# The first layer norm of a two-layer network in pairs of row tiles, with another order of the products behind it

## The reference, cut to what matters

```python
def _layernorm(x, axis=-1, eps=1e-05):
    m = jnp.mean(x, axis=axis, keepdims=True)
    v = jnp.var(x, axis=axis, keepdims=True)
    return (x - m) / jnp.sqrt(v + eps)
...
x = L0_attn_x
xn = _layernorm(x, axis=-1)
s = _L0_attn_ref(xn, ...)                 # q, k, v projections, softmax attention
g = _silu(_L0_ffn_ref(xn, ...))           # 16 experts, the top 4 of each row
x = x + s * g
...                                       # a second layer of the same build
```

## Time and profile before

| what | value |
|---|---|
| time, median of 3 runs | 410.19 us (410.18 to 410.86) |
| the profiled execution | 410.36 us |
| its span, first to last instruction | 408.6 us |
| TensorE busy | 392.9 us, 96% |
| VectorE, ScalarE, GpSimd busy | 315.1, 231.4, 210.3 us |
| chain that ended last | TensorE 85%, VectorE 11% |

### The profile page before, as it was taken

One profiled execution on the slowest core, in us unless ns is written; L12 is line 12 of the kernel. 1 busy time (PEld: TensorE's weight loads), 2 busy tenths in 40 slices (PEclk: granted clock), 3 DMA queues, 4 the chain that ended last, 5 costly groups with the idle time before them and its releaser, 6 DMA issues.

```text
span 408.6 us, 9640 instructions
## 1 busy us (share of the span) xinstructions
PE 392.9 (96%) x3063; PEld 289.1 (71%) x3063; DVE 315.1 (77%) x1070; ACT 231.4 (57%) x583; POOL 210.3 (51%) x205
## 2 busy tenths in 40 slices
PE   8999999999999999999899899999999999999995
PEld 4846797797787787566576677468778776566784
DVE  5895888888897556698999988766877862645895
ACT  3463334434344446899999943645777767524731
POOL 1214487776763210486878410177777620677710
PEclk9999999999999999999999999999999999999999
DMA  6949789899999997288788973034656544233322
GB/s 214 391 205 319 249 294 300 277 296 314 291 321 290 309 316 254 64 191 231 137 207 206 270 263 131 13 92 130 197 178 189 163 150 135 80 104 103 91 72 70
DMA packets 41361, 82.84 MB, mean 203 GB/s; under 512 B 6960, under 2 KB 26288, under 8 KB 40672
## 3 DMA queue, kind: packets, MB, share of 16 engines
q1 hardware_dynamic: 30080, 60.59, 44.3%
q0 software_dynamic: 9600, 19.93, 19.4%
q10 hardware_dynamic: 1632, 1.71, 1.3%
HBM read 65.42 MB, written 14.68 MB: 196 GB/s over the span
## 4 chain that ended last, share of the span: by engine, by line
PE 85%; DVE 11%; issue 3%; ACT 1%; ACTq 0%; DVEq 0%
PE ps L1261 13%; PE ps L1200 8%; PE ps L1485 7%; PE ps L1300 6%; PE ps L1406 5%; PE ps L1227 5%; PE ps L1379 4%; PE ps L1496 3%; PE ps L1256 3%; PE ps L1186 3%; PE ps L1029 3%; PE ps L1048 2%; PE ps L1045 2%; PE ps L1238 2%; PE ps L1387 2%
## 5 line engine op out<-in xcount | busy, mean ns | idle before, releaser
L592 POOL DMA_INDIRECT til<-xn_rows,gidx x64 | 62.5, 976 | 82.7 <-PE ps L1238 37.2
L915 ACT ACTIVATE til<-til,mxs 128x128 f32<-128x128 f32 (+1 forms) x128 | 48.9, 451 | 0.0
L1261 PEld LDWEIGHTS ps<-til,experts 128*128 128x128 f32 x384 | 45.4, 192 | 4.2 <-DVE til L1832 2.4
L1261 PE MATMUL ps<-til,experts 128*128 128x128 f32 x384 | 47.7, 277 | 0.4 <-DVE til L1832 0.3
L767 ACT ACTIVATE til<-ps 128x256 f32<-128x256 f32 x40 | 15.3, 382 | 56.5 <-PE ps L1238 55.6
L1956 DVE CUSTOM_DVE_ANT_0 til<-ps,cst 128x128 f32<-128x128 f32 (+1 forms) x128 | 37.9, 354 | 5.2 <-PE ps L1379 4.5
L816 ACT ACTIVATE til<-ps,wtile 128x256 f32<-128x256 f32 x88 | 38.7, 469 | 4.3 <-PE ps L1229 2.4
L1202 PE MATMUL ps<-xn,til 128*64 128x192 f32 x192 | 33.8, 329 | 0.0
L1200 PE MATMUL ps<-experts,til 128*64 x192 | 33.7, 329 | 0.0
L1300 PE MATMUL ps<-experts,til 128*128 x128 | 33.1, 381 | 0.0
L1406 PE MATMUL ps<-cst,til 128*128 128x128 f32 x192 | 27.5, 280 | 4.2 <-DVE til L1965 3.0
(11 more groups left out here) (278 smaller groups left out, 1034.8 us busy)
## 6 DMA issues: line engine op xcount, KB each, us to landing
experts<-in_gu SPq DMA_DIRECT2D x32, 512.0 KB, 5.4
sorted_rows<-til SPq DMA_DIRECT2D x88, 128.0 KB, 4.2
att<-in_gu SPq DMA_DIRECT2D x16, 512.0 KB
experts<-in_gu SPq DMA_DIRECT2D x8, 768.0 KB
experts<-in_dn SPq DMA_DIRECT2D x4, 1024.0 KB, 11.2
experts<-in_dn SPq DMA_DIRECT2D x8, 384.0 KB
experts<-att SPq DMA_DIRECT2D x44, 32.0 KB
xn_rows<-xn ACTq DMA_DIRECT2D x8, 128.0 KB, 4.8
```

The lines of the kernel that those rows point to most:

```text
L592: po.indirect_dma_start(to, None, xn_dram[s.n], bass.IndirectOffsetOnAxis(ap=gidx[:, at:at + 1], axis=0))\
L915: ins = ac.activation(pr[h % len(pr)][:, cols], pr[h % len(pr)][:, cols], ACT.Exp, bias=mxs[:, h % len(pr), tt:tt + 1], scale=-1.0)
L1261: mm = pe.matmul(ps[:, b0, m * P:(m + 1) * P], gw[n][:, k * w + m * P:k * w + (m + 1) * P], xgT[:, j % 2, k, :], start=(k == 0), stop=(k = ...
```

## The change

The norm of the first layer goes by pairs of tiles. VectorE takes the statistics of the next pair between the moments of a pair and its normalisation, the last two pairs being written out apart. Epsilon is no longer added by VectorE: it is a column of its own (`eps`, set by a new memset ahead of `ones_bf`) that ScalarE adds as the bias of its root, read straight from the variances. ScalarE takes four roots of two tiles in place of two of four; the second, third and fourth stand behind its copies of tiles 0, 2 and 3. On TensorE 11 products of ones run in place of 16, `router(3)` stands ahead of `narrow(0)` and `turn(4)`, and `narrow(6)` ahead of `count(3)`. The table's first use writes to a scratch column instead of `rstd`.

```diff
@@ scalar
-            ac.wait_ge(s_dve, 1)
-            ac.activation(rstd[:, 0:1], ones_e[:, 0:1], ACT.Sqrt)
+            ac.wait_ge(s_dve, 2)
+            ac.activation(ahead[:, :], ones_e[:, 0:1], ACT.Sqrt)
...
+                    def deviations(b):
+                        ac.wait_ge(s.ve_ready, b + 1)
+                        ac.activation(sd[:, 2 * b:2 * b + 2], mv[:, 2 * b:2 * b + 2, 1], ACT.Sqrt, bias=eps[:, :]).then_inc(s.sd_ready, 1)
+
+                    deviations(0)
                     for i in range(NTT):
-                        if i % 4 == 0:
-                            ac.wait_ge(s.ve_ready, i // 4 + 1)
-                            ac.activation(sd[:, i:i + 4], sd[:, i:i + 4], ACT.Sqrt).then_inc(s.sd_ready, 1)
                         turned(s, i)
+                        if i in (0, 2):
+                            deviations(i // 2 + 1)
+                        if i == 3:
+                            deviations(3)
@@ tensor
                         if i == 4:
+                            router(s, 3)
                             narrow(s, 0)
                         if i < NTT:
                             turn(s, i)
-                        if i >= 1:
+                        if i >= 1 and i != 4:
                             router(s, i - 1)
...
                     narrow(s, 5)
+                    narrow(s, 6)
                     count(s, 3)
-                    narrow(s, 6)
                     narrow(s, 7)
...
-            dense(16, 2)
+            dense(11, 2)
@@ vector
+            def pair_stats(b):
+
+                if b < len(X_PARTS):
+                    ve.wait_ge(s_x[b], 16)
+                for i in (2 * b, 2 * b + 1):
+                    ins = ve.bn_stats(bnst[:, i, :], xr[:, i, :])
                 link(ins)
...
+            def pair_moments(b):
+
+                for i in (2 * b, 2 * b + 1):
                     ins = ve.bn_aggr(mv[:, i, :], bnst[:, i, :])
...
+                ins.then_inc(L[0].ve_ready, 1)
+
+            def pair_normal(b):
+
+                ve.wait_ge(L[0].sd_ready, b + 1)
+                link(ve.reciprocal(rstd[:, 2 * b:2 * b + 2], sd[:, 2 * b:2 * b + 2]))
+                ve.wait_ge(L[0].ve_ready, b + 1)
+                for i in (2 * b, 2 * b + 1):
                     ve.tensor_scalar(xn[:, i, :], xr[:, i, :], mv[:, i, 0:1], rstd[:, i:i + 1], ALU.subtract, ALU.mult)\
-                      .then_inc(s.xn_ready, 1)
+                      .then_inc(L[0].xn_ready, 1)
...
             link(ve.memset(ones_e[:, :], 1.0))
+            link(ve.memset(eps[:, :], EPS))
             ve.memset(ones_bf[:, :], 1.0).then_inc(s_cbf, 1)
-            variances(L[0], 0)
-            rows_normal(L[0], 0, 4, 1)
-            variances(L[0], 1)
-            rows_normal(L[0], 4, NTT, 2)
+            pair_stats(0)
+            pair_moments(0)
+            for b in (0, 1):
+                pair_stats(b + 1)
+                pair_normal(b)
+                pair_moments(b + 1)
+            pair_stats(3)
+            pair_moments(3)
+            pair_normal(2)
+            pair_normal(3)
```

More of the change, by code:

```diff
@@ L239, in build_program @@
         bnst = sb("bnst", [P, NTT, 6])
+        eps = sb("eps", [P, 1])
         mv = sb("mv", [P, NTT, 2])
@@ L1577, in _ @@
             done = {}
[L1579 to L1585, removed]
+            def pair_stats(b):
[3 more added lines that the diff above has]
+                    ins = ve.bn_stats(bnst[:, i, :], xr[:, i, :])
                 link(ins)
-                for i in range(4 * h, 4 * h + 4):
+            def pair_moments(b):
+                for i in (2 * b, 2 * b + 1):
                     ins = ve.bn_aggr(mv[:, i, :], bnst[:, i, :])
[L1589 to L1596, removed]
+                ins.then_inc(L[0].ve_ready, 1)
[4 more added lines that the diff above has]
+                for i in (2 * b, 2 * b + 1):
                     ve.tensor_scalar(xn[:, i, :], xr[:, i, :], mv[:, i, 0:1], rstd[:, i:i + 1], ALU.subtract, ALU.mult)\
-                      .then_inc(s.xn_ready, 1)
+                      .then_inc(L[0].xn_ready, 1)
             def picks(s, p):
```

## The result

The changed kernel took 416.87 us (median of six executions, 413.93 to 419.96) against 410.19 before: a ratio of 1.0151, with a 95% interval of 1.0116 to 1.0186, which is 4.8 to 7.6 us slower. The direction was forecast; 412.2 was not reached by any execution, and the median lies 3 us above the range. The six executions of this one program are 6 us apart (413.93, 414.51, 414.70, 419.04, 419.92, 419.96), while those of before lay within 0.8 us. The mean granted clock is 0.990 to 0.996 in the three faster ones and 0.977 to 0.978 in the three slower. The profiled execution is the fastest, 413.93 (span 412.1, and 1.8 around it). Of the runs further down, two executions in the chip's slower state, 567 us of e10 and 453 us of the kernel before beside it, are left out of every median.

The account below looks back on a forecast made before the run. TensorE, busy 96% of the span, was taken as the bound: 1.1 us later at `narrow(1)` plus 0.86 for `narrow(6)` made 410.36 + 1.96 = 412.32, less 0.17 for the median: 412.2 us, range 410.6 to 413.9.

Parts of the forecast that it names:

- Starvation and order: Late rows and TensorE's new order delay `narrow(1)` about 1.1 us, `narrow(6)` adds 0.86: 1.96 us; chance 0.63.
- the hinge: End of `count(3)` on TensorE, which starts `nts` at 18.97; any delay there delays everything behind it equally.
- The range of this case: Main forecast of waits and order on TensorE: 1.3 to 2.6 us slower, given as 411.5 to 412.9 us.
- the two stops at the routers: TensorE waits 0.2 us before `router(3)` and 0.4 us before `router(4)` in the new order.
- The root with a bias: ScalarE's first root, bounded by 0.20 and 0.39 us, ends before VectorE needs it, so it is hidden.
- Rival 2: Tile 2 reaches TensorE by about 7.1, so TensorE is not starved: 409.9 us, or within 0.2%; chance 0.20.
- The warming products: Before TensorE's first turn: eleven products run from 1.36 to about 5.8 us, where sixteen ended at 6.68.
- Part 2: With eleven products TensorE is free for tile 0 at 6.02 and turns it at 6.09, 0.68 us earlier.
- rival 1: TensorE's clock rises later or falls again after fewer products and idle time: up to 1.5 us more, 413.7; chance 0.17.
- The sign that the prediction named for this: Router or `narrow` rows between 8 and 13 us spaced twice as far as before would mean the clock.
- Near 20.9: Start of `nts` on VectorE after the change, in place of 18.97, with VectorE idle about 2.3 us before it.

Follow-up runs that it names:

- e10: Changed kernel with rows in four transfers, second root before ScalarE's first copy, TensorE's old order, 11 products plus 4 after `turn(1)`: 409.81 us, ratio 0.9989.
- e1: Changed kernel with 16 warming products in place of 11, all else as changed: 412.61 us, ratio 1.0056.
- e4: Changed kernel's pairs and bias with 16 warming products and TensorE's order of before: 411.27 us, ratio 1.0016.
- e7: Kernel before with only `narrow(6)` moved ahead of `count(3)`: 411.12 us, ratio 1.0016.
- e8: Changed kernel with 16 products and rows fetched in four transfers, the third ahead of the identity matrix: 413.10 us, ratio 1.0059.
- e9: Kernel before with 11 products, plus 24 products of 16 columns before the first turn and 16 between `turn(1)` and `router(0)`: 414.94 us, ratio 1.0083.
- e6: Kernel before with its 16 products divided, 11 ahead of the first turn and 5 between `turn(1)` and `router(0)`: 411.87 us, ratio 1.0009.
- e2: Kernel before with 11 warming products in place of 16, nothing else: 417.38 us, ratio 1.0151.
- e0: The changed kernel once more, unaltered, on another chip: 418.31 us, ratio 1.0169.
- e5: Changed kernel with its 11 products plus four more between `router(0)` and `turn(2)`: 412.75 us, ratio 1.0058.

## Why the prediction was half right

**Starvation and order: right.** Point by point in the trace of after: VectorE idles 0.74 us before its third statistics (0.65 forecast) because of the transfer of rows; the third tile is turned at 8.63 (8.66); the last choice, at 18.28, ends before TensorE is there, so `narrow(6)` lies in front of the hinge. e1 has the sum without the clock, 2.3 us by its ratio (1.6 to 3.0) for 1.96 forecast. (The range of this case, +1.3 to +2.6 on 410.19, ends at 412.8 and not at 412.9; nothing hangs on it.) e4 and e7 have two of its parts, 0.7 us each by their ratios (0.1 to 1.3, and none to 1.3), for 0.54 and 0.86, though the clock fell in both profiles and is mixed into these times; the two stops at the routers, 0.55 by the forecast, were not tried alone.

**The root with a bias: right.** ScalarE's row of after, against the earlier trace rows:

```profile
4.70 0.29 ACT L725 ACTIVATE sd<-mv,eps 128x2 f32<-128x2 f32 x1 [2.48 <-DVE mv L1598]
```

0.29 us, in the middle of the bounds 0.20 and 0.39, and hidden. That the later roots are hidden too held only while the rows came late, as e8 shows. Rival 2 (rows in time, not slower) had left that root out: in e8 the rows came in time, and the second pair's reciprocal still began only at 8.69.

**The warming products: wrong.** Part 2 set down their removal as "TensorE is free when tile 0 comes", a gain of 0.68 us at its place, and the sum gave it no cost; its price was left to rival 1, at 0.17. That is the step that failed. Rival 1 had named what happened ("the level could rise later, or fall again"), but three of its terms were off:

- Its chance was low because "the eleven products do outlast the moment at which the level rose here". That moment was read off one execution and is not fixed: it came at 4.1 us in e9, 5.4 in before, 7.1 in e7, and behind 9.8 in e6. In the changed kernel itself the eleven products did not outlast it, as the load at 5.15 and the slow turns at 6.10 show.
- Its price was bounded by the 4.2 us that the clock took to rise at the start. The level stayed low for 13.6 us in e2 and for about 17 in e0.
- Its cause, idle time, is at most a part: in e2 the level stayed low while the profile shows TensorE busy throughout.

The sign was right because the two losses add. Of the 6.2 us (by the ratio), e1, which has the five products back, keeps 2.3; the remaining 4 go with the five products. The same five taken from the kernel before cost 6.2 (4.6 to 7.8, e2).

The sign that the prediction named for this, `narrow` rows at twice their length, is what the trace of after shows at 10.63. "Near 20.9" for `nts` was refuted by 1.3 us, and the whole of it is there at `narrow(1)` already (16.23 for 14.95), behind the rows that ran at half the speed.

**What stays open.** That the missing products cost the time is shown (e2, e1, e5). What about them holds the level isn't settled. With eleven alone it fell in each of the three profiles (after, e0, e2); with four more in a pause it held (e5, e10); with sixteen it held past 24 us in all but one profile (e4); with short products it held until 14 us (e9). Idle time, the kind of work and the moment of the rise all vary between these runs, and no run varied one with the others fixed. The moment of the rise is not the kernel's to choose, so part of what one profile shows is luck; the times of several executions are the firmer evidence. Sixteen are no guarantee either (e4).

## What to carry to other kernels

Products that only warm TensorE are paid for by what comes long after them: before taking some away because "TensorE waits there anyway", look at what work follows, and compare the lengths of equal rows (a `narrow`, a router) in several executions, not one. Find the one wait at which two engines' chains meet, and ask of each edit whether it moves that point; a filler put ahead of it costs its full length. When a small step (a root) is cut into more steps, look at what stands ahead of each in its engine's queue: a wait that is removed on one side uncovers the one behind it.

## What the runs showed of the hardware

- TensorE can be busy 100% by the profile for 13 us and stay at 1.2 GHz (e2, 9 to 22 us, fp32 turns of 128 columns, routers of 16, then `narrow` of 256), and the level can fall right behind 3 to 3.5 us without a pause (e4, e9). The busy share of the page doesn't tell whether the level will hold. The Trainium skill ("TensorE: Matmul & The Clock Gate", Part 1) puts the return of the low level down to idleness of TensorE. The stretches of e4 and e9 show a fall behind a busy share of 1.00, so that share at least is no measure of such idleness; it counts the time with an instruction under way, and no run here shows how full the engine was in it.
- The moment at which the level first rises is not the same in every execution. The products of ones start at 1.2 to 1.3 us in all profiles, and their weight loads, 0.43 us apart from the third on, first come closer at 4.1 (e9), 5.4 and 7.1 us (e7); in e6 all sixteen products, up to 9.8 us, ran at the lower level.
- One program at one place of its execution took 413.9 to 420.0 us, with mean granted clocks of 0.996 to 0.977; the profiles of its fastest execution and of e0's slowest differ by how long the level was low. The mean can miss a loss, however: two executions of e2 took 417.54 and 417.66 us with a mean of 1.0 listed. In the profiles the level is listed as 1.00 until its first recorded change, though products run at half speed there; that those two rose late is an inference, since no trace of them exists.
